# Second attention of a two-layer cross-attention kernel: all low parts of the probabilities on GpSimd, value banks copied out by VectorE, stacked operands through a pre-stacked scratch

## Chip, cores and metric

The kernel runs on one core of a Trainium2 chip. The metric is the device time of one execution in microseconds; a profiled execution gives the trace.

## What is computed

Two layers, each an attention and an MLP, for 4 batches of 512 tokens of width 512, 16 heads of 32. The change lies in the attention of the second layer alone:

```python
h = jnp.concatenate([x, latents], axis=1)               # 64 context rows + 512 latents
q = (latents @ q_w + q_b).reshape(b, k_len, NH, DH)
kv = (h @ kv_w + kv_b).reshape(b, p + k_len, NH, DH, 2)
kmat, v = (kv[..., 0], kv[..., 1])
attn = jnp.einsum('bkhd,bnhd->bhkn', q, kmat) / DH
attn = jnp.where(full_mask[:, None, None, :], attn, -jnp.inf)
attn = jax.nn.softmax(attn.astype(jnp.float32), axis=-1).astype(q.dtype)
attn_out = jnp.einsum('bhkn,bnhd->bkhd', attn, v).reshape(b, k_len, H)
attn_out = attn_out @ out_w + out_b + residual
```

## The kernel before

Every fp32 operand of a matmul is split into a high part, rounded to the matmul's type, and a low part, the difference from it; a product is made of three matmuls (high by high, high by low, low by high). For scores the split is stacked along the contraction: rows 0 to 31, 32 to 63 and 64 to 95 of `QS` hold high, high and low of a head's Q, those of `KS` high, low and high of its K, so that one matmul makes all three products. Row 96 is the mask, row 97 (`ROWMAX`) the row's maximum, which thus is subtracted by the same matmul.

The second attention (`attention1` on each engine) walks over 4 batches; a batch has 4 groups `c` of 4 heads, a group 20 steps: 4 heads by 5 key tiles (4 of 128 keys and one of 64 context keys). Steps are numbered `n` in the batch, `i` in the group. In step `n` TensorE issues

- `scores(n)`: the scores of step n, transposed (keys on partitions), into bank 4 or 5. At `i == 0` it waits for `maxed`, the DMA of the row of maxima of its group;
- `max_step`: one or two matmuls of scores of the *next* group, whose maxima over the keys VectorE takes (banks 2 and 3; steps 2 to 15 of a group). The first of each pair of heads waits for `stacked`, the loads of `QS` and `KS`;
- `values(n - 4)` (`LAG`): two matmuls of the value product of an earlier step, of the high part `ph` and the low part `pl` of its probabilities, into bank 6 or 7; one head's output is summed there over five steps. The low part it waits for by `p_lo` (VectorE) or `p_lo_pool` (GpSimd);
- a slice of the projections for the group after the next (`fillers`: Q, K, K of the context; in the second group also the transposes of the next batch's tokens).

ACT makes `exp(n)` twice from the bank, rounded into `ph` and in fp32 into `pf`, both rings of five (`PRING`); before it overwrites them it waits for the low part and the value matmul of step n - 5. The low part `pl = pf - ph` is made by GpSimd where `lo_by_pool(n)` says so (key tiles 1 and 3, and the context tile of even heads, 10 of 20 steps) and by VectorE (`lo_p`) otherwise.

When a head is finished, ACT (`o_out(h)`, one step behind the last value matmul) copies rows 0 to 64 of its bank into `sg`, VectorE (`o_sum(h)`) adds the high and the low half into `oa` and frees the bank, and SyncE (`sums(h)`) moves row 64, the sum of the probabilities, into `s16` by DMA.

SyncE issues all these DMAs in an order written out in `attention1.batch` for each group: the sums of the last head before, the parts of Q to the scratch `q_parts` in HBM (`parts(0, ...)`), a sums row, the parts of K (`parts(1, ...)`), the first half of the stacked loads (`pair(0)`, two heads), a sums row, the row of maxima (`max_row`, line 550), the second half of the stack (`pair(1)`), a sums row. The loads are for the group two further on. One half of a stack is three loads of 32 rows for Q and three for K (line 543), and for two of the four groups a mask row (line 546). The row of maxima comes from VectorE's join of two tables of maxima (line 1510), a transpose on TensorE (line 1950, issued in step 17) and a copy by VectorE (line 1517).

In the last batch, from step 40 on, GpSimd also loads and splits eight blocks of MLP weights, one every five steps (lines 696 to 711), in the same instruction stream as its low parts (line 841). In the last group of every batch it adds the bias row to four residual tiles (line 854).

Of the kernel before, what the change touches and what calls it, by code (L numbers as in the profile page):

```python
# [26 lines left out]
F32 = mybir.dt.float32  # L27
# [3 lines left out]
ACT = mybir.ActivationFunctionType  # L31
# [140 lines left out]
def lo_by_pool(i):  # L172

    j, t = STEPS[i % NSTEP]
    return t in (1, 3) or (t == TT and j % 2 == 0)
# [14 lines left out]
STACK = 16 * 13  # L190


def stack_count(c):
    return 16 * 7 if c < 2 else STACK
# [8 lines left out]
def program(nc, x, ctx, mask_bool, mask_int, w, x1, xm, x2, q_parts, k_parts, out):  # L203
# [4 lines left out]
    with es:  # L208
# [126 lines left out]
        pv_step = sem("pv_step")  # L335
        sg_ready = sem("sg_ready")
        o_free = sem("o_free")
# [110 lines left out]
        def _(sp):  # L448
# [77 lines left out]
            def attention1():  # L526
                src, dst = tokens(xm), tokens(x2)

                def parts(x, nb, c):

                    for half in range(2):
                        wait_apart(sp, (stacked[c % 2][half], at(0, nb, STACK, stack_count(c - 2) if c >= 2 else 0)))
                    sp.dma_start((q_parts, k_parts)[x][c % 2], (qt, kt)[x].bitcast(F32)).then_inc(parted[x][c % 2], 16)

                def stack(nb, c, half):

                    to = stacked[c % 2][half]
                    heads = slice(2 * half, 2 * half + 2)
                    for x, dst_, src_, order_ in ((0, QS, q_parts, (0, 0, 1)), (1, KS, k_parts, (0, 1, 0))):
                        wait_apart(sp, (parted[x][c % 2], at(0, nb, 32, 16 * (c // 2 + 1))))  # L540
                        rows_of = src_[c % 2].rearrange("(j p) h n -> p j h n", p=HD)
                        for r, part in enumerate(order_):
                            sp.dma_start(dst_[r * HD:(r + 1) * HD, c % 2, heads, :].bitcast(F32),
                                         rows_of[:, heads, part, :]).then_inc(to, 16)
                    if c < 2:
                        sp.dma_start(KS[ROWMASK:ROWMASK + 1, c % 2, heads, S:NK].bitcast(F32),
                                     kbias[0:1, 1, ds(nb * C, C)].bitcast(F32).unsqueeze(1).to_broadcast([1, 2, C]))\
                            .then_inc(to, 16)
# [8 lines left out]
                def batch(b, last):  # L557
                    def sums(h):
                        sp.wait_ge(sg_ready, at(0, b, H, h + 1))
                        sp.dma_start(s16[h:h + 1, :], sg[2 * HD:2 * HD + 1, h % 2, :])\  # L560
                            .then_inc(o_moved[h % 2], 16)
# [6 lines left out]
                    for c in range(G):  # L568
# [8 lines left out]
                        if last and c == G - 1:  # L577

                            wait_apart(sp, (pb_full, at(0, b, USES, use1(f"R{G - 1}", last) + 1)),
                                       (parted[0][1], at(0, b, 32, 32)), (parted[1][1], at(0, b, 32, 32)))  # L580
# [11 lines left out]
                        if ahead:  # L592
                            wait_apart(sp, (pb_free, at(0, b, USES, use1(f"{pre}KC{nc_}", last) + 1)))
                            parts(1, nb, nc_)
                            pair(0)
# [5 lines left out]
                        if ahead:  # L601
                            pair(1)
                        sums(HG * c + 2)
# [275 lines left out]
        def _(act):  # L879
# [167 lines left out]
            def attention1():  # L1047
# [5 lines left out]
                def hi(b, u, last=False, first=False):  # L1053

                    kind = u.lstrip("n")
                    if kind[0] in "QK":
# [3 lines left out]
                        if not (first and c == 0):  # L1060
                            wait_apart(act, (parted["QK".index(kind[0])][(c + 1) % 2],
                                             at(0, own, 32, 16 * ((c - 1) // 2 + 1) if c else 0)))
# [23 lines left out]
                def batch(b, last):  # L1086
# [19 lines left out]
                    def o_out(h):  # L1106
                        wait_apart(act, (pv_step, at(0, b, BSTEP, (h + 1) * (TT + 1))),
                                   (o_moved[h % 2], at(0, b, 128, 16 * (h // 2))), (o_free, at(0, b, H, h - 1)))
                        act.activation(sg[0:2 * HD + 1, h % 2, :], bank[6 + h % 2][0:2 * HD + 1, :], ACT.Copy)\
                            .then_inc(sg_ready, 1)  # L1110

                    for c in range(G):
                        at_step = {s0 + n: u for s0, n, u in fillers(c, last)}
                        for i in range(NSTEP):
# [4 lines left out]

                            h, t = divmod(n - LAG - 1, TT + 1)  # L1120
                            if t == TT and h >= 0:
                                o_out(h)
# [7 lines left out]
                    o_out(H - 1)  # L1130
# [58 lines left out]
        def _(dve):  # L1189
# [278 lines left out]
            def attention1():  # L1468
# [50 lines left out]
                def batch(b, last):  # L1519
# [10 lines left out]
                    def o_sum(h):  # L1530
                        j = h % HG
                        dve.wait_ge(sg_ready, at(0, b, H, h + 1))
# [611 lines left out]
```

## Time and profile before

| | before |
|---|---|
| median of 3 runs | 1864.66 us (1859.7 to 1866.77) |
| profiled execution | 1862.46 us, span 1860.6 |
| PE, DVE, ACT, POOL busy, share of the span | 88%, 54%, 38%, 29% |
| mean granted TensorE clock | 0.93 |
| second attention, first score to last value matmul | 766.4 to about 1436 us |

Engines are named as the profile names them: PE is TensorE, PEld its weight loads, DVE VectorE, ACT ScalarE, POOL GpSimd, SP SyncE (SPq its DMA queue). Times are microseconds from the span's start. In groups by line, "x" is a count, then the busy time, the mean of one, the idle time just before and what ended it. In the timeline, square brackets hold the idle time before an instruction and what released it. A shape is partitions x elements, output first.

### The profile page before, as it was taken

How to read it: one execution, taken by the hardware profiler on the slowest of the kernel's cores; microseconds unless marked ns; L12 is line 12 of the kernel's file. 1: busy time of each engine (PE TensorE's matmuls, PEld its weight loads, DVE VectorE, ACT ScalarE, POOL GpSimd, SP SyncE). 2: the span in 40 equal slices, each digit the busy share in tenths (PEclk: the TensorE clock that was granted, in tenths of full speed). 3: DMA queues.
4: the chain of work that ended last, by engine and by line, in shares of the span. 5: the costliest groups of instructions: out<-in, count | busy, mean ns of one | idle time of the engine just before them, and what ended most of it. 6: DMA issues, size and time to landing. Idle time of an engine off the chain costs nothing.

```text
span 1860.6 us, 23089 instructions
## 1 busy us (share of the span) xinstructions
PE 1642.2 (88%) x6993; PEld 1229.6 (66%) x6993; DVE 1009.4 (54%) x1612; ACT 703.4 (38%) x1260; POOL 541.9 (29%) x543
## 2 busy tenths in 40 slices
PE   5778887899999998888988898989886699999998
PEld 4667775667878786555665555655553477787886
DVE  3665565554333335667766766775787455334333
ACT  3433333431111111367556745663667232111111
POOL 2232245404040505133323422341358210404000
PEclk9788898999999998789988999998988799999999
DMA  5011023501010215223123223221221420101011
GB/s 176 1 40 63 23 91 100 177 1 46 0 45 0 91 70 186 68 83 112 61 72 94 87 61 109 65 91 61 95 84 46 151 81 1 46 0 45 0 41 50
DMA packets 60730, 126.13 MB, mean 68 GB/s; under 512 B 10397, under 2 KB 10722, under 8 KB 60642
## 3 DMA queue, kind: packets, MB, share of 16 engines
q1 hardware_dynamic: 53602, 102.08, 16.8%
q0 software_dynamic: 7040, 23.07, 4.1%
q8 instruction: 31, 0.51, 0.1%
q14 instruction: 57, 0.47, 0.1%
HBM read 90.25 MB, written 34.60 MB: 67 GB/s over the span
## 4 chain that ended last, share of the span: by engine, by line
PE 70%; DVE 14%; issue 6%; ACT 4%; DMA 3%; SPq 1%; POOL 0%; ACTq 0%; DVEq 0%; POOLq 0%
PE bank L2064 18%; PE bank L2052 17%; PE bank L1926 5%; DVE RA L1268 4%; PE bank L1961 3%; PE bank L1922 3%; PE bank L2023 3%; DVE FA L1501 3%; PE bank L1976 3%; PE bank L1977 2%; PE bank L1939 2%; PE bank L1748 2%; PE bank L1724 2%; PE bank L1943 2%; PE bank L1799 1%
## 5 line engine op out<-in xcount | busy, mean ns | idle before, releaser
L2064 PE MATMUL bank<-W,RA 128*128 128x512 f32 x1536 | 384.3, 402 | 25.3 <-DVE RA L1268 25.1
L2052 PE MATMUL bank<-RA,W 128*128 (+1 forms) x1536 | 374.7, 396 | 2.7 <-issue 2.3
L2064 PEld LDWEIGHTS bank<-W,RA 128*128 128x128 f32 x1536 | 290.3, 191 | 99.5 <-DVE RA L1268 31.2
L841 POOL TENSOR_TENSOR RA<-FA,RA 128x512 fp32r<-128x512 f32 (+1 forms) x160 | 216.0, 1354 | 423.9 <-ACT FA L1104 423.8
L2052 PEld LDWEIGHTS bank<-RA,W 128*128 128x128 f32 x1536 | 286.9, 188 | 74.9 <-issue 5.9
L1268 DVE TENSOR_TENSOR RA<-FA,RA 128x512 fp32r<-128x512 f32 (+2 forms) x308 | 274.7, 894 | 68.0 <-ACT FA L1104 54.5
L1160 ACT ACTIVATE FA<-bank,cols 128x512 f32<-128x512 f32 x128 | 88.2, 689 | 560.2 <-PE bank L2052 560.1
L1631 DVE CAST RA<-FA 128x512 fp32r<-128x512 f32 x128 | 62.5, 488 | 368.9 <-ACT FA L1160 368.7
L1103 ACT ACTIVATE RA<-bank 128x512 fp32r<-128x512 f32 (+1 forms) x320 | 192.4, 601 | 170.3 <-PE bank L1961 164.6
L1501 DVE TENSOR_REDUCE FA<-bank 128x1 f32<-128x512 f32 x256 | 169.1, 685 | 65.4 <-PE bank L1939 64.1
L1104 ACT ACTIVATE FA<-bank 128x512 f32<-128x512 f32 (+1 forms) x320 | 191.5, 599 | 0.0
L1961 PE MATMUL bank<-RA 98*128 98x512 f32 (+1 forms) x320 | 144.7, 454 | 37.5 <-DMA RA<-rows_ 29.7
L1926 PE MATMUL bank<-RA,W 128*128 128x512 f32 (+1 forms) x576 | 147.9, 375 | 5.3 <-DVE FA L1491 2.9
L1976 PE MATMUL bank<-RA 128*65 128x512 f32 (+1 forms) x320 | 140.5, 439 | 8.8 <-DVE RA L1268 5.2
L1268 DVE TENSOR_TENSOR RA<-bank,RA 128x512 fp32r<-128x512 f32 (+1 forms) x124 | 82.9, 680 | 114.2 <-ACT RA L1084 43.5
L1977 PE MATMUL bank<-RA 128*65 128x512 f32 (+1 forms) x320 | 135.1, 422 | 0.0
L1926 PEld LDWEIGHTS bank<-RA,W 128*128 128x128 f32 x576 | 99.7, 200 | 42.0 <-issue 14.1
L1961 PEld LDWEIGHTS bank<-RA 98*128 98x128 f32 (+1 forms) x320 | 62.8, 197 | 83.2 <-issue 45.6
L700 POOL TENSOR_TENSOR W<-raw,W 128x512 fp32r<-128x512 f32 (+1 forms) x88 | 110.2, 1252 | 7.4
L1661 DVE TENSOR_TENSOR FA<-bank,FA 128x512 f32 (+1 forms) x128 | 86.2, 689 | 37.8 <-PE bank L2064 37.2
L1939 PE MATMUL bank<-RA 97*128 97x512 f32 x256 | 100.3, 432 | 2.3 <-DVE FA L1501 1.8
L696 POOL TENSOR_SCALAR W<-raw 128x512 fp32r<-128x512 f32 (+1 forms) x88 | 55.1, 626 | 62.7 <-DMA raw<-in_L_xattn_mlp_w_dram 20.5
(149 smaller groups left out, 1838.1 us busy)
## 6 DMA issues: line engine op xcount, KB each, us to landing
RA<-k_parts SPq DMA_DIRECT2D x96, 144.0 KB
FA<-after_layer SPq DMA_DIRECT2D x12, 1024.0 KB, 6.2
RA<-q_parts SPq DMA_DIRECT2D x96, 128.0 KB
k_parts<-FA SPq DMA_DIRECT2D x16, 576.0 KB, 3.2
after_att<-FA SPq DMA_DIRECT2D x32, 256.0 KB, 2.1
q_parts<-FA SPq DMA_DIRECT2D x16, 512.0 KB, 2.7
raw<-in_L_xattn_mlp_w_dram POOLq DMA_DIRECT2D x32, 256.0 KB, 3.4
RA<-after_att SPq DMA_DIRECT2D x12, 512.0 KB, 8.6
```

Of the source, the lines that this page charges most:

```text
L841: pool.tensor_tensor(pl[0:m, r, :], pf[0:m, r, :], ph[0:m, r, :].bitcast(F32), ALU.subtract).then_inc(p_lo_pool, 1)
L1103: act.activation(ph[0:m, r, :], src, ACT.Exp, scale=SCALE1)
L1104: act.activation(pf[0:m, r, :], src, ACT.Exp, scale=SCALE1).then_inc(p_exp, 1)
L1268: dve.tensor_tensor(dst, src, hi.bitcast(F32), ALU.subtract).then_inc(sem_, 1)
L1501: dve.tensor_reduce(nm_main[:, TT * j + t:TT * j + t + 1], bank[2 + i % 2][:, :], AX_X, ALU.max, negate=True).then_inc(mm_free, 1)
L1926: op = pe.matmul(dst[:, 0:m], W[:, "QK".index(kind[0]), a, k, c * P:(c + 1) * P], src[:, d, k, :], start=start, stop=stop)
L1939: pe.matmul(bank[2 + i % 2][:, :], QS[0:ROWMAX, c % 2, j, t * P:(t + 1) * P], KS[0:ROWMAX, c % 2, j, 0:S], start=True, stop=True).then_inc ...
L1961: pe.matmul(bank[4 + n % 2][0:m, :], KS[0:ROWMAX + 1, c % 2, j, t * P:t * P + m], QS[0:ROWMAX + 1, c % 2, j, :], start=True, stop=True).th ...
L1976: pe.matmul(o, v, ph[0:m, n % PRING, :], start=(t == 0), stop=False)
L1977: pe.matmul(o, v, pl[0:m, n % PRING, :], start=False, stop=(t == TT)).then_inc(pv_step, 1)
L2052: op = pe.matmul(bank[FC1_BANK[i]][:, :], W[:, slot, a, k, i * P:(i + 1) * P], yT_[:, ds(b * (2 * KT * S) + (d * KT + k) * S, S)], start=( ...
L2064: op = pe.matmul(bank[4 + t][:, :], gs[:, a, i, t * P:(t + 1) * P], W[:, slot + 1, d, i, :], start=(i == 0 and a == 0 and d == 0), stop=(i ...
```

## The change

In the second attention:

- `lo_by_pool` is true for every step: GpSimd makes all 320 low parts, VectorE none;
- the copy of a finished head's bank into `sg` moves from ACT (`o_out` is removed) to VectorE, into `o_sum`, ahead of its addition;
- the scratch holds Q and K stacked already: `parts` writes three copies (high, high, low for Q; high, low, high for K) with three DMAs instead of both parts with one, and `stack` loads 96 rows with one DMA for Q and one for K instead of three each. The counts that are waited for follow (48 instead of 16 on `parted`, 3 or 2 loads of 16 on `stacked` where there were 7 or 6);
- in SyncE's order `pair(0)` moves behind `sums(HG * c + 1)` and `max_row`, and `pair(1)` behind `sums(HG * c + 2)`.

```diff
 def lo_by_pool(i):
     j, t = STEPS[i % NSTEP]
-    return t in (1, 3) or (t == TT and j % 2 == 0)
+    return True
...
-STACK = 16 * 13
+STACK = 16 * 5
 def stack_count(c):
-    return 16 * 7 if c < 2 else STACK
+    return 16 * 3 if c < 2 else STACK
...
                     for half in range(2):
                         wait_apart(sp, (stacked[c % 2][half], at(0, nb, STACK, stack_count(c - 2) if c >= 2 else 0)))
-                    sp.dma_start((q_parts, k_parts)[x][c % 2], (qt, kt)[x].bitcast(F32)).then_inc(parted[x][c % 2], 16)
+                    to = (q_parts, k_parts)[x][c % 2]
+                    for r, part in enumerate(((0, 0, 1), (0, 1, 0))[x]):
+                        sp.dma_start(to[:, r, :, :], (qt, kt)[x][:, part, :].bitcast(F32)).then_inc(parted[x][c % 2], 16)
...
-                    for x, dst_, src_, order_ in ((0, QS, q_parts, (0, 0, 1)), (1, KS, k_parts, (0, 1, 0))):
-                        wait_apart(sp, (parted[x][c % 2], at(0, nb, 32, 16 * (c // 2 + 1))))
-                        rows_of = src_[c % 2].rearrange("(j p) h n -> p j h n", p=HD)
-                        for r, part in enumerate(order_):
-                            sp.dma_start(dst_[r * HD:(r + 1) * HD, c % 2, heads, :].bitcast(F32),
-                                         rows_of[:, heads, part, :]).then_inc(to, 16)
+                    for x, dst_, src_ in ((0, QS, q_parts), (1, KS, k_parts)):
+                        wait_apart(sp, (parted[x][c % 2], at(0, nb, 96, 48 * (c // 2 + 1))))
+                        sp.dma_start(dst_[0:3 * HD, c % 2, heads, :].bitcast(F32),
+                                     src_[c % 2, heads].rearrange("j r p n -> (r p) j n")).then_inc(to, 16)
...
                             parts(1, nb, nc_)
-                            pair(0)
                         sums(HG * c + 1)
                         if not (last and c == G - 1):
                             u = f"R{c + 1}" if c + 1 < G else "nR0"
                             wait_apart(sp, (pb_free, at(0, b, USES, use1(u, last) + 1)))
                             max_row(b if c + 1 < G else b + 1, (c + 1) % G)
                         if ahead:
+                            pair(0)
+                        sums(HG * c + 2)
+                        if ahead:
                             pair(1)
-                        sums(HG * c + 2)
...
-                    def o_out(h):
-                        wait_apart(act, (pv_step, at(0, b, BSTEP, (h + 1) * (TT + 1))),
-                                   (o_moved[h % 2], at(0, b, 128, 16 * (h // 2))), (o_free, at(0, b, H, h - 1)))
-                        act.activation(sg[0:2 * HD + 1, h % 2, :], bank[6 + h % 2][0:2 * HD + 1, :], ACT.Copy)\
-                            .then_inc(sg_ready, 1)
...
                     def o_sum(h):
                         j = h % HG
+                        dve.wait_ge(pv_step, at(0, b, BSTEP, (h + 1) * (TT + 1)))
+                        wait_apart(dve, (o_moved[h % 2], at(0, b, 128, 16 * (h // 2))))
+                        dve.tensor_copy(sg[0:2 * HD + 1, h % 2, :], bank[6 + h % 2][0:2 * HD + 1, :]).then_inc(sg_ready, 1)
                         dve.wait_ge(sg_ready, at(0, b, H, h + 1))
...
-    parts = [nc.dram_tensor(n, (2, P, 2, m), F32, kind="Internal").ap() for n, m in (("q_parts", S), ("k_parts", NK))]
+    parts = [nc.dram_tensor(n, (2, HG, 3, HD, m), F32, kind="Internal").ap() for n, m in (("q_parts", S), ("k_parts", NK))]
```

## Rows read from the trace of the kernel before

**Rows 1.** Busy time by stretch (window, length, then each engine, clock, DMA)
```profile
948.40:1087.50 139.10, 121.61 (x530) 81.26 (x530) 103.65 (x159) 98.53 (x191) 57.43 (x43) 0.94 0.29 90
...
981.90:1020.80 38.90, 35.18 (x149) 23.95 (x149) 25.47 (x40) 25.35 (x50) 12.85 (x10) 0.88 0.24 72
```

**Rows 2.** Waits of TensorE, 766 to 1440: total us, times, longest
```profile
PE bank L1961 <- DMA RA<-rows_: 29.7, 11, 3.9
PE bank L1943 <- DVE FA L1501: 23.1, 27, 2.0
...
PE bank L1903 <- DVE FA L1491: 7.9, 6, 1.6
```

**Rows 3.** VectorE by line and shape, 766 to 1440
```profile
L1501 DVE TENSOR_REDUCE FA<-bank 128x1 f32<-128x512 f32 x240 | 158.3, 685 | 64.4 <-PE bank L1939 63.5
L1268 DVE TENSOR_TENSOR RA<-FA,RA 128x512 fp32r<-128x512 f32 x140 | 144.0, 1031 | 46.8 <-ACT FA L1104 41.4 <-ACT RA L1144 4.9
L1533 DVE TENSOR_TENSOR FA<-bank,FA 32x512 f32<-32x512 f32 x64 | 43.8, 684 | 3.9 <-ACT FA L1109 2.1
```

**Rows 4.** ACT's copy of a value bank: ns min/median/max, first and last start
```profile
L1109 ACT ACTIVATE FA<-bank x64: 582/584/682, 785.7 to 1436.4; 65x512 f32<-65x512 f32 x64
```

**Rows 5.** Timeline of low parts: start, us, engine, line, operation, count
```profile
954.79 2.53 POOL L841 TENSOR_TENSOR RA<-FA,RA 128x512 fp32r<-128x512 f32 x2 [0.78 <-ACT FA L1104]
...
958.82 1.29 POOL L841 TENSOR_TENSOR RA<-FA,RA 128x512 fp32r<-128x512 f32 x1 [1.51 <-ACT FA L1104]
958.89 1.77 DVE L1268 TENSOR_TENSOR RA<-FA,RA 128x512 fp32r<-128x512 f32 x1
...
1433.73 1.26 POOL L841 TENSOR_TENSOR RA<-FA,RA 128x512 fp32r<-128x512 f32 x1
```

**Rows 6.** Timeline of SyncE's DMA queue at a group's end
```profile
1047.90 1.63 SPq L543 DMA_DIRECT2D RA<-q_parts  x3
...
1052.63 0.53 SPq L560 DMA_DIRECT2D FA<-FA  x1
1053.35 0.56 SPq L551 DMA_DIRECT2D RA<-rows_  x1
1054.17 1.30 SPq L543 DMA_DIRECT2D RA<-q_parts  x3
```

**Rows 7.** Timeline of VectorE and TensorE at group ends and starts
```profile
1049.52 0.28 DVE L1517 CAST rows_<-bank 16x128 fp32r<-16x128 f32 x1
...
1055.29 0.76 PE L1961 MATMUL bank<-RA 98*128 98x512 f32 x1 [3.85 <-DMA RA<-rows_]
...
1020.86 0.47 PE L1961 MATMUL bank<-RA 98*128 98x512 f32 x1 [0.41 <-DMA RA<-rows_]
...
1023.50 0.40 PE L1939 MATMUL bank<-RA 97*128 97x512 f32 x1
...
1372.45 0.77 PE L1961 MATMUL bank<-RA 98*128 98x512 f32 x1 [3.31 <-DMA RA<-rows_]
```

**Rows 8.** Busy time in one slice, with the DMA share and GB/s last
```profile
1058.00:1059.00 1.00, 1.00 (x4) 0.81 (x3) 0.01 (x1) 0.64 (x2) 0.19 (x1) 0.50 0.56 124
```

**Rows 9.** The page's DMA issues: count, KB each, us to landing
```profile
k_parts<-FA SPq DMA_DIRECT2D x16, 576.0 KB, 3.2
```

**Rows 10.** GpSimd by line, 1370.4 to 1435.1, the last batch's second half
```profile
L841 POOL TENSOR_TENSOR RA<-FA,RA 128x512 fp32r<-128x512 f32 (+1 forms) x21 | 29.8, 1428 | 5.0 <-ACT FA L1104 5.0
L700 POOL TENSOR_TENSOR W<-raw,W 128x512 fp32r<-128x512 f32 x8 | 11.7, 1464 | 0.7
L854 POOL TENSOR_TENSOR FA<-FA,brow 128x512 f32<-128x512 f32 x4 | 6.5, 1617 | 0.0
L696 POOL TENSOR_SCALAR W<-raw 128x512 fp32r<-128x512 f32 x8 | 5.0, 629 | 4.0 <-DMA raw<-in_L_xattn_mlp_w_dram 3.8
L711 POOL DMA_DIRECT2D raw<-in_L_xattn_mlp_w_dram x7 | 4.1, 584 | 0.0
```

**Rows 11.** The join of maxima: ns min/median/max, first and last start
```profile
L1510 DVE TENSOR_TENSOR FA<-FA x16: 175/175/178, 763.3 to 1398.8; 128x16 f32<-128x16 f32 x16
```

## What the change will do to the time

> **What bounds the kernel now.** The second attention is the stretch from 766 to 1440 us: four batches of 80 steps, 20 steps to a group of four heads, then the batch's tail (value projections, normalising, output projection). I read it in four views. The first is the table of busy time by stretch [rows 1]: the reader is to see that in the 139.1 us of one batch's steps TensorE is busy 121.6, VectorE 103.7 and GpSimd only 57.4. TensorE is thus the engine nearest to full, but part of its busy time is slow time: the group from 981.9 shows a granted clock of 0.88. Of the two levels (1.0 and 0.5 of full, 2.4 and 1.2 GHz) that is 24% of 38.9 us, 9.3 us, at the lower one; at full clock the same work would have taken some 4.6 us less.
>
> The second view, who TensorE waited for [rows 2], tells what interrupts it: the row maxima that come by DMA (29.7 us in 11 waits, always the first score of a group), and VectorE (23.1 and 7.9 us) where a bank of maxima or of a projection was not yet drained. The third, VectorE by line and shape [rows 3], says why VectorE is late: its low parts of the probabilities (both inputs in SBUF) take 1031 ns on the mean, while instructions of the same size that read PSUM take 685. The timeline shows the cause [rows 5]: a GpSimd low part begins at 958.82 for 1.29 us, a VectorE one at 958.89 needs 1.77 and ends 0.55 after GpSimd's. The fourth view is the timeline of the queues at a group's end [rows 6, 7].
>
> **The change, part by part.**
>
> *Low parts.* VectorE gives up 160 of 320, 40 a batch; at 1.0 us (128 rows, by [rows 3]) that is 40 us of its 103.7. GpSimd takes them. Two back to back took 2.53 us [rows 5], so 1.27 each when VectorE doesn't interfere, and nothing of VectorE's steps would now have two large SBUF inputs. 80 a batch are 101.6 us, and four residual additions of the same size 5.1: 106.7 us in 139. By the step, GpSimd needs 1.27 (1.52 in a batch's last group) where a step lasts 1.74 on the mean (139.1/80). A step's low part is due four steps later, about 6 us; score, two exponentials and 1.27 make some 3. So in the first three batches GpSimd keeps up, and what hides the longer instruction is the lag of four steps. The cover is thin in a group's last four steps, which carry no maxima and run at ACT's pace of about 1 us: there GpSimd falls back 4 x 0.3 us and recovers at the next group's start. Taken as nothing to +4 us in all.
>
> *Copying out.* The 64 copies of the value banks move from ACT (584 ns each, 37 us, [rows 4]) to VectorE. The trace has no such copy on VectorE; nearest is its addition that reads the same bank, 684 ns [rows 3], so 11 us a batch. VectorE's sum: 103.7 - 40 + 11 = 75 of 139 us. The copy waits for the value matmul and for the earlier sums row to have left by DMA; behind it in VectorE's queue stand the next maxima, for which TensorE would wait. Both signals belong to work two or more steps older, so the wait should be over on arrival. Value: 0, between 0 and +5.
>
> What TensorE gains: of the 31 us that it waited for VectorE [rows 2] I take two thirds, 20, since VectorE goes from 75% to 54% busy. Bounds: 5 (waits set by bursts of two maxima, not by load) to 35 (all of it and some clock).
>
> *SyncE's queue.* Before, at the group's end at 1047.9, the queue issued three Q stack loads, waited for the K scratch, issued three K loads and the mask rows, then a sums row at 1052.63, and only at 1053.35 the row of maxima [rows 6], though VectorE had that row at 1049.80 (1049.52 + 0.28) [rows 7]. TensorE stood for 3.85 us until 1055.29. After, the queue reaches the maxima before the stack: issue at about 1050.0, and the score could start 1.94 later as before (1055.29 - 1053.35), at 1051.9 instead of 1055.3. TensorE's own work ended at 1051.44, so some 0.5 us of wait stay.
>
> The first half of the stack, moved past that row, now starts at about 1050.6 instead of 1047.9. The second half in the trace was issued at 1054.17 [rows 6], and its bytes ended in the slice 1058 to 1059, which is 0.56 busy, so about 4.4 us later [rows 8]. The first half would land at 1055.0. Who waits for it: the first matmul of maxima in the next group, which stood 2.6 us behind the group's first score at full clock (1020.86 to 1023.50, [rows 7]); so it is due at 1054.5. A new wait of about 0.5 us takes the place of 3.85, a net gain of 2.9. Of the 11 waits three or four (the group in which the tokens are transposed, 0.41 at 1020.86) have nothing to give, and lose up to 0.5. Eight give on the mean 2.6: 20 us. Bounds: nothing (the stack lands 3 us later than that) to 30. The second half moves past one sums row alone, and its due time is six or more steps off: 0.
>
> *Scratch and stack DMAs.* Q and K are written to the scratch in three copies rather than two parts (3 issues for 1, half as many bytes more), and each stack load is 1 issue for 3 with the same bytes. One K write of 576 KB landed in 3.2 us [rows 9]; 864 KB would need 4.8 by proportion, but it is issued four or five steps ahead of the stack in its new place, and the buffer that it frees is refilled a group later. Value 0; bounds -2 to +6. The same at the start of the stage: two more issues, hidden by VectorE's set-up: 0 to +2.
>
> *The last batch* is where GpSimd has no room. From step 40 on it also splits eight weight blocks. The window from 1370.4 to 1435.1 [rows 10] shows 29.8 us of low parts in 21 instructions, 11.7 and 5.0 of splits, 6.5 of residual, 4.7 of DMA issue (seven in 4.1, and an eighth alike), 3.8 of waiting for the first block, and only 5.0 us idle. After: 40 x 1.27 = 50.8; 8 x 1.27 = 10.2; 5.0; 4 x 1.27 = 5.1; 4.7; 3.8: together 79.6 us. Before, step 40's score stood at 1372.45 [rows 7]; its low part, now the first in the line, can start some 1.7 us later (0.77 and two ACT instructions of about 0.5). 1374.1 + 79.6 = 1453.7, against 1435.0 for the last GpSimd low part before (1433.73 + 1.26, [rows 5]). Nothing covers that: values, sums and the tail follow it. +19 us. Bounds: +12 (half the first block's wait and the start hidden) to +28 (1428 and 1464 ns an instruction as now, [rows 10]).
>
> The Trainium skill (GPSIMD Engine Reference, section Engine selection) speaks against the move: for an elementwise operation on two inputs it wants VectorE, GpSimd being about twice as slow. The rows agree on the instruction, 1.27 against about 0.69, but which engine has the time to spare decides here, and that is GpSimd outside the last 40 steps.
>
> **Sum**, against the profiled execution (1862.46, span 1860.6, 2.2 below the median of 1864.66): -20 (waits for VectorE) - 20 (group ends) + 19 (last batch) = -21, 1841.5 for such an execution, or 1844 by the median.
>
> **Rivals.**
> 1. *GpSimd becomes the pace in all four batches* (slower). If a low part takes 1.62 us, as the residual additions do on the mean among VectorE's traffic [rows 10], a batch's 84 instructions take 136 us, and with some 3 us before its first low part as long as the steps take now (139): the gains of all batches are gone, and the last 40 steps cost +28: 1892. It decides from about 1.5 us an instruction, where 84 of them and the 3 us pass the 129 that the steps need after the gains. Against it: back to back they took 1.27, and the interfering instructions leave.
> 2. *The stack load takes the place of the row of maxima* (no change). If the one large load lands 3 us later than computed, each group waits at its first maxima as long as it did at its first score: the 20 us of the group ends are gone, 1864. For it: the K half must wait for three scratch copies, 4.8 us by proportion.
> 3. *More comes free* (faster). VectorE's waits go wholly, and TensorE, with no idle of 3 us at group ends, keeps its clock: 5 us more a batch: 1864 - 20 - 20 + 19 - 20 = 1823.
> 4. *GpSimd blocks the joining of maxima* (no change). The join reads two SBUF tiles and stands on the path to the row of maxima. In the trace it took 175 to 178 ns all 16 times [rows 11], never blocked; but GpSimd was half idle. With GpSimd always running, each join could wait the rest of an instruction, up to 1.27, on the mean 0.6 us, 15 times, and VectorE's queue with it: +10 us, 1854. The Trainium skill (SBUF — State Buffer, section SBUF: two separate sides) says that such an instruction and a GpSimd one exclude each other for their whole length; the pair at 958.8 agrees.
>
> **How the numbers follow.** Chances: forecast 0.49, rival 1 0.12, rival 2 0.20, rival 3 0.13, rival 4 0.06. Predicted: 1844. The range takes rivals 3, 4 and 2 with some of their own width: 1820 to 1872; rival 1 and the ends stay out. About 0.5% (9.3 us) is what a measurement of this kernel can tell: faster is below 1855, with the forecast and rival 3, 0.62; same, rivals 2 and 4, 0.26; slower, rival 1, 0.12.
>
> **What would show it.** Right: TensorE's waits for the row of maxima fall from 29.7 to under 10 us; its waits for VectorE's reductions to under 12; VectorE shows no instruction of over 1 us in the steps; the low parts on GpSimd come at 1.27; the step part of a middle batch takes 126 to 130 us instead of 139; the last 40 steps of the last batch take 78 to 84 us instead of 63. A wait for a stack load of over 2 us at every group speaks for rival 2, a GpSimd instruction mean of over 1.5 us for rival 1, joins of over 0.5 us for rival 4. Wrong would be a step part that stays at 139 with GpSimd named as what TensorE waits for.

## The result, and the profile after

The kernel became slower. Its median is 1963.74 us (1962.45 to 1967.65, 4 runs), that of the kernel before, run beside it, 1862.88 (1859.7 to 1866.77): a ratio of 1.0544, with a 95% interval of 1.0517 to 1.0571. The forecast was 1844 within 1820 to 1872. The profiled execution has a span of 1961.4 us, 100.8 more than before, and a mean granted clock of 0.896 where it was 0.930.

I split the span at the first score of the stage, at the last batch's first score and its step 40, and at the last value matmul:

| us | start to first score | first three batches | last batch, 40 steps | last 40 steps | behind it | span |
|---|---|---|---|---|---|---|
| before | 766.4 | 536.9 | 69.1 | 63.5 | 424.7 | 1860.6 |
| after | 782.7 | 592.8 | 77.8 | 81.6 | 426.5 | 1961.4 |

The loss lies in every batch (56 us in the first three) and at the start (16), and only 18 of it in the last 40 steps, where GpSimd was expected to be late. The first view is who TensorE waited for, from 760 to 1560 us (total us, times, longest), which answers [rows 2]:

```profile
PE bank L1953 <- DMA RA<-rows_: 94.2, 13, 9.9
PE bank L1968 <- POOL RA L841: 16.7, 12, 2.2
...
PE bank L1942 <- DVE FA L1499: 7.1, 12, 1.7
...
PE bank L1935 <- DVE FA L1490: 3.1, 12, 0.3
```

The wait for VectorE's reductions (now line 1935, 23.1 us before) is gone. The wait for the row of maxima, which the change was to shorten, went from 29.7 us in 11 to 94.2 in 13. The second view shows one of the 13, in the timeline of SyncE's queue (start, us, line, operation, count), which answers [rows 6]:

```profile
1005.68 2.17 SPq L535 DMA_DIRECT2D k_parts<-FA  x3
1007.98 1.78 SPq L560 DMA_DIRECT2D FA<-FA  x1
1009.95 0.59 SPq L551 DMA_DIRECT2D RA<-rows_  x1
1010.88 0.35 SPq L543 DMA_DIRECT2D RA<-q_parts  x1
1019.64 0.32 SPq L543 DMA_DIRECT2D RA<-k_parts  x1
```

and the matching line of TensorE (in brackets the idle time before, and what ended it):

```profile
1020.05 0.77 PE L1953 MATMUL bank<-RA 98*128 98x512 f32 x1 [9.93 <-DMA RA<-rows_]
```

The order is the one intended: the row of maxima is issued at 1009.95, ahead of the stack. But it lands 10.1 us after its issue, not 1.9 as in [rows 6, 7]; and the K half of the stack, which waits for the three scratch copies issued from 1005.68, is issued at 1019.64, 14.0 us after them. One copy of 576 KB, two thirds of these bytes, took 3.2 us before [rows 9]. K's loads wait for the copies in the program; the row of maxima waits for nothing once it is issued, and still landed only when the copies had. The third view is the table of busy time by stretch, with the columns of [rows 1], within that wait, just behind it, and over the first three batches; below it three rows to compare with, two of the kernel before (behind the 3.85 us wait of [rows 7], and its first three batches) and one of the kernel after with the old scratch, an experiment below (its first three batches):

```profile
1016.00:1017.00 1.00, 0.00 (x0) 0.00 (x0) 0.00 (x0) 0.00 (x0) 0.00 (x0) 0.50 0.25 86
...
1020.00:1025.00 5.00, 4.95 (x12) 3.28 (x13) 0.30 (x1) 2.80 (x6) 2.55 (x2) 0.50 0.82 211
1025.00:1030.00 5.00, 5.00 (x24) 3.43 (x23) 2.38 (x4) 2.76 (x6) 3.08 (x3) 0.98 0.19 46
...
782.70:1375.40 592.70, 476.54 (x1956) 320.61 (x1957) 285.24 (x464) 305.04 (x573) 320.43 (x252) 0.86 0.28 85
```

```profile
1055.30:1060.30 5.00, 5.00 (x13) 3.38 (x14) 1.06 (x2) 2.86 (x6) 1.49 (x2) 0.55 0.62 164
...
766.40:1303.30 536.90, 473.30 (x1956) 317.95 (x1957) 360.07 (x536) 325.84 (x621) 180.42 (x132) 0.91 0.26 81
```

```profile
762.30:1288.10 525.80, 471.44 (x1957) 315.73 (x1958) 284.67 (x464) 302.46 (x573) 319.34 (x252) 0.92 0.26 83
```

The last but one column is the share of 16 DMA engines: while every compute engine stands and the copies alone are under way, it is 0.25 (0.26 from 1014 to 1018), four engines of sixteen. The column before it is the clock: TensorE stands, and the first 5 us of the next group run at the lower level (0.50), with 12 matmuls where the next 5 us see 24. That looks like a second cost, but most of it isn't new: behind the 3.85 us wait the first 5 us had a clock of 0.55 and 13 matmuls. Over three batches TensorE was busy for 476.5 us, 473.3 before: of the 55.8 us more, 3.2 are busy time. Against the kernel after with the old scratch, which has every other part of the change, it is 5.1 of 66.9; the rest is standing.

Why four engines: the scratch before is one contiguous block of 128 rows; after, `to[:, r, :, :]` picks one of three parts of each of four heads, so that the HBM side of a copy is 4 blocks of 32 rows that can't be merged. The Trainium skill (DMA: Bandwidth & Descriptors, section "Why a DMA increments its semaphore by 16 and not by 1") says that a DMA is spread over the largest number up to 16 that divides the slowest dimension of both sides: 16 for 128 rows, 4 for 4 blocks. The share of 0.25 agrees; the experiments test it at 4 and at 2 on the kernel before.

At the stage's start and in the batch tails the same thing shows. The first Q and K copies, in the queue's timeline after and then before:

```profile
721.49 1.81 SPq L535 DMA_DIRECT2D q_parts<-FA  x3
723.49 8.67 SPq L535 DMA_DIRECT2D k_parts<-FA  x3
735.52 0.35 SPq L543 DMA_DIRECT2D RA<-q_parts  x1
```

```profile
724.62 0.34 SPq L533 DMA_DIRECT2D q_parts<-FA  x1
725.15 0.32 SPq L533 DMA_DIRECT2D k_parts<-FA  x1
729.60 1.26 SPq L543 DMA_DIRECT2D RA<-q_parts  x3
```

From the first copy's issue to the first stack load are 14.0 us instead of 5.0, and issuing K's copies alone held the queue for 8.67. In the three tails between batches VectorE's reciprocal waits 14.5 us in all for the sums rows (last row of the next view; in the fourth it waits for none), and each of them takes 37.5 us from the last value matmul to the next first score, where it took 31.1 to 31.2. VectorE by line and shape, which answers [rows 3]:

```profile
L1523 DVE COPY FA<-bank 65x512 f32<-65x512 f32 x64 | 43.5, 679 | 34.7 <-PE bank L1969 30.0 <-DMA FA<-FA 4.6
L1499 DVE TENSOR_TENSOR FA<-FA 128x16 f32<-128x16 f32 x16 | 5.6, 348 | 0.5
L1563 DVE RECIPROCAL FA<-FA 16x512 f32<-16x512 f32 x4 | 13.4, 3344 | 14.6 <-DMA FA<-FA 14.5
```

GpSimd did what was forecast; its low parts (ns minimum, median, maximum), answering [rows 5]:

```profile
L841 POOL TENSOR_TENSOR RA<-FA,RA x320: 1251/1281/1455, 786.3 to 1533.1; 128x512 fp32r<-128x512 f32 x128, 64x512 fp32r<-64x512 f32 x32
```

### The profile page after: what moved, and what is told of

Its sections match the earlier page's. It is cut to its first block, busy times and chain, and to the rows that moved or that the text cites. A ratio compares the mean times of both kernels' runs of the same rounds, so it can differ in the third digit from the quotient of the medians.

```text
span 1961.4 us, 23079 instructions
## 1 busy us (share of the span) xinstructions
PE 1660.7 (85%) x6993; PEld 1237.9 (63%) x6993; DVE 903.9 (46%) x1516; ACT 677.1 (35%) x1196; POOL 725.0 (37%) x703
## 4 chain that ended last, share of the span: by engine, by line
PE 65%; DVE 10%; DMA 9%; issue 6%; ACT 4%; POOL 2%; SPq 2%; DVEq 0%; POOLq 0%; ACTq 0%
PE bank L2056 17%; PE bank L2044 16%; PE bank L1918 6%; DMA RA<-rows_ 5%; PE bank L1953 3%; PE bank L1968 3%; PE bank L1931 3%; PE bank L2015 3%; PE bank L1969 2%; DVE RA L1257 2%; DMA k_parts<-FA 2%; PE bank L1716 2%; PE bank L1740 2%; POOL RA L841 2%; PE bank L2009 1%
## 5 line engine op out<-in xcount | busy, mean ns | idle before, releaser
L841 POOL TENSOR_TENSOR RA<-FA,RA 128x512 fp32r<-128x512 f32 (+1 forms) x320 | 406.8, 1282 | 338.8 <-ACT FA L1104 334.0
L2056 PEld LDWEIGHTS bank<-W,RA 128*128 128x128 f32 x1536 | 291.5, 192 | 100.0 <-DVE RA L1257 31.1
L2044 PEld LDWEIGHTS bank<-RA,W 128*128 128x128 f32 x1536 | 287.1, 188 | 75.2 <-issue 6.2
L1953 PE MATMUL bank<-RA 98*128 98x512 f32 (+1 forms) x320 | 148.8, 467 | 100.3 <-DMA RA<-rows_ 94.2
L1968 PE MATMUL bank<-RA 128*65 128x512 f32 (+1 forms) x320 | 147.0, 459 | 16.9 <-POOL RA L841 16.7
L1969 PE MATMUL bank<-RA 128*65 128x512 f32 (+1 forms) x320 | 140.9, 440 | 0.0
L1918 PEld LDWEIGHTS bank<-RA,W 128*128 128x128 f32 x576 | 104.4, 208 | 51.3 <-issue 14.0
L1257 DVE TENSOR_TENSOR RA<-FA,RA 128x512 fp32r<-128x512 f32 (+1 forms) x148 | 113.4, 768 | 13.0 <-ACT RA L1133 6.5
L1653 DVE TENSOR_TENSOR FA<-bank,FA 128x512 f32 (+1 forms) x128 | 86.2, 689 | 37.5 <-PE bank L2056 37.0
L1968 PEld LDWEIGHTS bank<-RA 128*65 128x65 f32 (+1 forms) x320 | 48.4, 151 | 55.3 <-POOL RA L841 37.1
```

The lines of the kernel that those rows point to most:

```text
L841: pool.tensor_tensor(pl[0:m, r, :], pf[0:m, r, :], ph[0:m, r, :].bitcast(F32), ALU.subtract).then_inc(p_lo_pool, 1)
L1257: dve.tensor_tensor(dst, src, hi.bitcast(F32), ALU.subtract).then_inc(sem_, 1)
L1918: op = pe.matmul(dst[:, 0:m], W[:, "QK".index(kind[0]), a, k, c * P:(c + 1) * P], src[:, d, k, :], start=start, stop=stop)
L1953: pe.matmul(bank[4 + n % 2][0:m, :], KS[0:ROWMAX + 1, c % 2, j, t * P:t * P + m], QS[0:ROWMAX + 1, c % 2, j, :], start=True, stop=True).th ...
L1968: pe.matmul(o, v, ph[0:m, n % PRING, :], start=(t == 0), stop=False)
L1969: pe.matmul(o, v, pl[0:m, n % PRING, :], start=False, stop=(t == TT)).then_inc(pv_step, 1)
```

## The experiments

Theory A: the loss is the shape of the scratch copies. Theory B: it is GpSimd, whatever the shape. Theory C: it is SyncE's new order. Every ratio below is against the kernel before, run on the same chip, with its 95% interval. No kernel leaves out part of the work.

**Low parts alone.** The kernel before with

```diff
-    return t in (1, 3) or (t == TT and j % 2 == 0)
+    return True
```

> The kernel before with one part of the change: GpSimd makes all 320 low parts; copies, scratch, stack loads and queue order as before. Theory A (the loss comes from the scratch copies, which the trace of after shows at about a quarter of the DMA engines: K's three copies are issued at 1005.68 and the stack load behind them can go at 1019.64, 14 us, while the DMA share stands at 0.13 to 0.3 and 50 to 110 GB/s): this part is harmless, some 20 us gained from VectorE and some 19 lost in the last batch, 1850 to 1870. Theory B (GpSimd's 1.28 us instructions are the pace): most of the 100 us, 1930 or more, with TensorE's waits for L841 in tens of us. Theory C (the new queue order is the loss): as A.

1848.66 us, ratio 0.9926 (0.9904 to 0.9948). Who TensorE waited for:

```profile
PE bank L1961 <- DMA RA<-rows_: 29.0, 10, 3.7
...
PE bank L1943 <- DVE FA L1501: 2.9, 11, 0.3
```

Alone, this part gains 15 us, a little more than I expected. By stretch (span 1849.0) the first three batches took 513.2 us instead of 536.9 and the last batch's first 40 steps 65.0 instead of 69.1; its last 40 took 80.2 instead of 63.5. So -28 and +17: GpSimd isn't the cause of the loss. Theory B falls. Not all of the 24 us in three batches is waiting: TensorE's busy time there fell from 473.3 to 463.5 us, at a granted clock of 0.92 instead of 0.91.

**The shape alone, on the kernel before.** One spare row in the scratch behind each 32, so that the same 128 rows and bytes are 4 blocks of 32; order and everything else stay (the loads' addresses follow, in a line that is left out here):

```diff
-    (q_parts, k_parts)[x][c % 2], (qt, kt)[x].bitcast(F32)
+    (q_parts, k_parts)[x][c % 2][:, 0:HD, :, :], (qt, kt)[x].bitcast(F32)
-    (2, P, 2, m)
+    (2, HG, HD + 1, 2, m)
```

> The kernel before with nothing of the change but the shape of its scratch copies: the scratch has one unused row behind each head's 32, so the same one copy of the same bytes goes out as 4 x 32 rows instead of 128. Theory A (a copy whose outermost size is 4 goes over 4 of the 16 DMA engines): the K copy lands in 9 to 10 us instead of 3.2 (864 KB took 14 us in the changed kernel, 576 KB is two thirds), each group's end waits some 6 us longer, 11 times, and the clock falls with it: 1925 to 1950. Theories B and C, and any theory in which the bytes or the number of copies matter: no change, 1860 to 1870.

1967.37 us, ratio 1.0564 (1.0533 to 1.0595): a loss as large as that of the whole change, from rows that nobody reads, and more than I had expected. SyncE's queue at a group's end and the wait of TensorE:

```profile
1055.01 0.57 SPq L533 DMA_DIRECT2D k_parts<-FA  x1
...
1065.39 1.24 SPq L543 DMA_DIRECT2D RA<-k_parts  x3
```

```profile
PE bank L1961 <- DMA RA<-rows_: 95.4, 13, 11.1
```

From the K copy to the stack's K loads are 10.4 us. In this order the row of maxima is late because SyncE stands ahead of it; in the kernel after, though it stands in front, because the copies' data do. The wait is the same, 95.4 and 94.2. The clock costs more here: the first three batches took 616.8 us instead of 536.9, and 15 of these 80 are TensorE's busy time (488.5 for 473.3, granted clock 0.86 for 0.91).

**The two controls.** A spare row behind each 64 (2 blocks, first edit), and one behind all 128 (still one block, second edit):

```diff
-    (2, P, 2, m)
+    (2, 2, 2 * HD + 1, 2, m)
...
+    (2, P + 1, 2, m)
```

> The kernel before with the unused scratch row behind each pair of heads, so that the one copy of the same bytes goes out as 2 x 64 rows. If the outermost size sets how many DMA engines take part (4 x 32 made K's copy last 10.4 us where 128 rows took 3.2): about twice 10.4, 19 to 21 us for K, some 10 us more at each of 15 group ends than with 4 x 32, 2090 to 2160. If it is the break in the addresses or the odd row: as with 4 x 32 or better, 1930 to 1970.

> The kernel before with one unused scratch row behind all 128, so that the copy stays 128 rows and only the scratch is larger. If the outermost size is the cause: 1855 to 1872, as before. If the scratch's size or place in HBM were: slower.

With the row at the end 1862.59 us, ratio 0.9993 (0.9976 to 1.0009); the K copy lands in 3.2 us:

```profile
k_parts<-FA SPq DMA_DIRECT2D x16, 576.0 KB, 3.2
```

With 2 blocks 2041.69, ratio 1.0963 (1.091 to 1.1016). Its queue, its DMA share (0.13, two engines of sixteen) and its wait:

```profile
1087.13 0.55 SPq L533 DMA_DIRECT2D k_parts<-FA  x1
...
1101.10 1.24 SPq L543 DMA_DIRECT2D RA<-k_parts  x3
```

```profile
1094.00:1098.00 4.00, 3.30 (x17) 1.49 (x15) 1.57 (x3) 4.00 (x9) 2.25 (x2) 1.00 0.13 53
```

```profile
PE bank L1961 <- DMA RA<-rows_: 142.8, 13, 15.1
```

So padding costs nothing. And one break in the block costs more than three: what counts is the number of blocks, not that of the breaks. The size was again off: I expected twice the time of 4 blocks; from the K copy to the stack's K loads are 14.0 us against 10.4.

**The change with the scratch and stack loads of before.** Low parts, copying out and order as after:

```diff
-                    to = (q_parts, k_parts)[x][c % 2]
-                    for r, part in enumerate(((0, 0, 1), (0, 1, 0))[x]):
-                        sp.dma_start(to[:, r, :, :], (qt, kt)[x][:, part, :].bitcast(F32)).then_inc(parted[x][c % 2], 16)
+                    sp.dma_start((q_parts, k_parts)[x][c % 2], (qt, kt)[x].bitcast(F32)).then_inc(parted[x][c % 2], 16)
...
-    (2, HG, 3, HD, m)
+    (2, P, 2, m)
```

> The changed kernel with the scratch and the stack loads of before (one copy of 128 rows with both parts, three loads of 32 rows for each half); GpSimd's low parts, VectorE's copy and the new queue order stay. Theory A: K lands in 3.2 us again, the row of maxima goes out ahead of the stack: what the prediction forecast, 1835 to 1860. Theory B: 1930 or more. Theory C: 1930 or more.

1862.40 us, ratio 1.0007 (0.9975 to 1.0038). The scratch's shape thus costs 1963.7 - 1862.4 = 101 us here, and 1967.4 - 1862.6 = 105 on the kernel before: theory A. Theory C falls too as the cause of the 101 us, since the new order is still in this kernel. But 1862 is just outside what I expected; without the shape the rest of the change gains nothing, though its low parts alone gain 15. Its waits, then the queue and the wait at one group's end:

```profile
PE bank L1931 <- DMA RA<-k_parts: 17.4, 8, 2.5
...
PE bank L1953 <- DMA RA<-rows_: 7.4, 9, 2.5
...
PE bank L1931 <- DMA RA<-rows_: 6.8, 3, 2.3
```

```profile
1039.89 0.55 SPq L551 DMA_DIRECT2D RA<-rows_  x1
1040.79 1.27 SPq L543 DMA_DIRECT2D RA<-q_parts  x3
1042.18 1.29 SPq L543 DMA_DIRECT2D RA<-k_parts  x3
1043.62 0.68 SPq L546 DMA_DIRECT2D RA<-rows_  x1
```

```profile
1046.39 0.50 PE L1931 MATMUL bank<-RA 97*128 97x512 f32 x1 [2.24 <-DMA RA<-rows_]
```

The first score (line 1953) hardly waits any more: 2.5 of its 7.4 us are at the stage's very first score, as before. Here it starts at 1041.83, 1.94 us after the row's issue, as before. The first matmul of maxima (line 1931) waits for the stack instead, K's loads or, where there is one, the mask row behind them (line 546, which the view names `rows_` too): 17.4 + 7.4 + 6.8 = 31.6 us, about what the row of maxima alone cost before (29.7).

**The stacked scratch, written in blocks of 32 rows.** The kernel after with each scratch copy cut by head: 12 issues of 32 rows, each contiguous, instead of 3 of 4 blocks:

```diff
-                        sp.dma_start(to[:, r, :, :], (qt, kt)[x][:, part, :].bitcast(F32))...
+                        for j in range(HG):
+                            sp.dma_start(to[j, r, :, :], (qt, kt)[x][j * HD:(j + 1) * HD, part, :].bitcast(F32))...
```

> The changed kernel with each scratch copy of 128 rows cut in four copies of 32 rows (12 issues for 3, the same bytes to the same places). Theory A: copies of 32 rows use all engines, K lands in 4 to 5 us; 12 issues take SyncE some 4.5 us instead of 2.2; waits for the row of maxima fall from 94 us to 10 to 30; 1845 to 1875. Theory B (GpSimd) and theory C (queue order): 1940 to 1965, since nothing of theirs changes.

1884.38 us, ratio 1.0119 (1.0075 to 1.0163): 79 of the 101 us come back with the same bytes in the same layout, a little less than I expected. The rest is 22 us over the run just above; the only things that differ are the 12 issues and half as many bytes more to the scratch, against one load instead of three. The 12 issues keep the queue for 5.46 us ahead of the row of maxima, and TensorE's waits for that row are 33.9 us, more than the 10 to 30 expected:

```profile
1012.38 5.46 SPq L536 DMA_DIRECT2D k_parts<-FA  x12
```

**Order alone, copying out alone**, on the kernel before. The edits are those of the diff above, `pair` moved in SyncE's order and `o_out` moved to VectorE.

> The kernel before with only SyncE's order changed (both halves of the stack behind the row of maxima and a sums row). If the order trades one wait for another (in the run with the old scratch the waits for the row of maxima were 4.9 us instead of 29, and 24.2 us of waits for stack loads stood in their place): 1860 to 1870, no difference beyond 0.5%. If the order gains what the prediction took for it: 1843. If the order is what made that run 13 us slower than low parts alone: 1872 to 1880.

> The kernel before with only the copy of a finished head's bank moved from ACT to VectorE. VectorE still makes its half of the low parts, so it gets 11 us a batch on top of 103.7: if the copy is hidden, 1860 to 1868; if VectorE's queue is close to its limit there, 1870 to 1885, with TensorE's waits for reductions above 23 us.

The order: 1875.84, ratio 1.0063 (1.0032 to 1.0094). The copy: 1881.26, ratio 1.0073 (1.004 to 1.0105). Both lose. Waits with the order alone, then with the copy alone:

```profile
PE bank L1940 <- DMA RA<-k_parts: 19.7, 8, 3.8
PE bank L1962 <- DMA RA<-rows_: 8.3, 10, 2.5
PE bank L1940 <- DMA RA<-rows_: 7.1, 3, 2.5
```

```profile
PE bank L1935 <- DVE FA L1490: 25.1, 38, 2.0
PE bank L1953 <- DMA RA<-rows_: 25.0, 12, 3.8
```

The order moves 21 us away from the first score (29.7 to 8.3) and puts 27 at the stack loads. What the copy costs on a VectorE that still makes half of the low parts isn't in one row of waits: that for a bank of maxima is only 2 us longer, in 38 instead of 27 pieces. It stands in TensorE's busy time: 488.9 us over the first three batches where it was 473.3, at a granted clock of 0.89 instead of 0.91; that is 15.6 of the 17.1 us by which they are longer. What lowered the clock wasn't tested.

**Each of the two beside the low parts.**

> The kernel before with GpSimd making all low parts and VectorE making the copies out; scratch, stack loads and order as before. The copy alone cost some 14 us, on a VectorE that still made its low parts. If that price is VectorE's load, it goes with the low parts: within 3 us of low parts alone, 1846 to 1853. If the copy costs by its place (ACT no longer paced by it, SyncE's sums rows later): 1858 to 1866.

> The kernel before with GpSimd making all low parts and the new order of SyncE's queue; copies, scratch and stack loads as before. The order alone cost some 12 us. If the stack loads behind the row of maxima are what costs, it costs the same here: 1858 to 1864, with 20 to 27 us of waits for stack loads. If it was VectorE's load that made the order dear: 1840 to 1850.

Low parts and copy: 1848.39, ratio 0.9935 (0.9914 to 0.9956), what the low parts gain alone (0.9926). Low parts and order: 1861.16, ratio 0.9995 (0.9969 to 1.002). So the copy is free once VectorE is relieved, and the order costs about 12 us on either base. Its waits:

```profile
PE bank L1940 <- DMA RA<-k_parts: 18.9, 8, 2.9
...
PE bank L1940 <- DMA RA<-rows_: 8.3, 3, 3.0
PE bank L1962 <- DMA RA<-rows_: 8.0, 10, 2.5
```

Over the whole stage they come to 35.2 us against 29.0 for low parts alone, 6 of the 12. The rest is again in TensorE's busy time: over the first three batches, 16.5 us longer in the profiled executions (529.7 for 513.2), it is 474.5 us instead of 463.5, at a granted clock of 0.91 instead of 0.92. Why stays open.

**The last 40 steps shared as before**, with the low parts on GpSimd everywhere else:

```diff
+    return not last or i < 2 * NSTEP or t in (1, 3) or (t == TT and j % 2 == 0)
```

> The kernel before with GpSimd making all low parts except in the last 40 steps of the last batch, where the old division between VectorE and GpSimd stays. If the 16 to 18 us that those 40 steps took longer (80.2 us with all low parts on GpSimd, 63.5 before) come from GpSimd's weight splits beside 40 low parts: 63 to 66 us again for them, 1830 to 1838 in all. If they come from something else (clock, norm work on VectorE): as the run with all low parts on GpSimd, 1845 to 1855.

1835.57 us, ratio 0.9844 (0.9807 to 0.9882). The first three batches took 513.8 us (513.2 with low parts alone), the last 40 steps 63.6, as before: the cost at the end and the gain elsewhere are two separate terms.

**Only the K loads pass the row of maxima.** That kernel, and in SyncE's order only the half that waits for the K scratch moved behind `max_row`; Q's three loads stay ahead and `pair(1)` stays where it was:

```diff
                             parts(1, nb, nc_)
-                            pair(0)
+                            pair(0, (0,))
                         sums(HG * c + 1)
...
                         if ahead:
+                            pair(0, (1,))
                             pair(1)
```

> As the run with the low parts shared at the end, and with the first half of the stack divided in SyncE's order: its Q loads stay where they were, its K loads (which wait for the scratch) go behind the row of maxima. If issue time and the wait for K's copy ahead of the row of maxima are what the 29 us of waits are made of: waits for that row fall to about 15, stack waits stay under 8, 1820 to 1833. If the stack then is as late as in the new order: no better than the run without it.

1811.99 us, ratio 0.9719 (0.9676 to 0.9762): faster than both kernels, 23.6 us faster than without the split on the same chip, and below the 1820 to 1833 that I expected. The queue and the wait:

```profile
1022.52 0.33 SPq L533 DMA_DIRECT2D k_parts<-FA  x1
1023.19 1.63 SPq L545 DMA_DIRECT2D RA<-q_parts  x3
1024.94 0.51 SPq L562 DMA_DIRECT2D FA<-FA  x1
1025.71 0.56 SPq L553 DMA_DIRECT2D RA<-rows_  x1
1026.38 1.45 SPq L545 DMA_DIRECT2D RA<-k_parts  x3
```

```profile
PE bank L1965 <- DMA RA<-rows_: 10.2, 9, 2.5
```

While the K copy lands, the queue issues what doesn't need it: Q's loads, a sums row, the row of maxima. K's loads then start 3.9 us after the copy's issue, with nothing left to wait for. The wait for the row falls from 28.4 us to 10.2, and those for the stack loads are 1.3 us in all. TensorE's busy time over the first three batches falls with it, from 463.9 us to 455.8, at a granted clock of 0.95 instead of 0.92: 8 of the 21 us gained there, which the expectation had left out. Two things differ from the order of the change, that Q's loads stay ahead and that `pair(1)` isn't moved; which of them counts more wasn't separated.

## Why the prediction was wrong, step by step

*What bounds the kernel*: right. TensorE, interrupted by the row of maxima at group ends and by VectorE's drained banks. Both waits moved when their causes were touched.

*Low parts*: right in the mechanism, and too careful by 8. Forecast -20 in the steps, all from waits; low parts alone gave 536.9 - 513.2 = 24 in three batches and 4 in the last one's first half. But 10 of the 24 are TensorE's busy time at a better clock, which the forecast had kept for its third rival: that the size is near is in part luck. 1.27 us an instruction was forecast, 1.28 came; the wait for reductions was to fall below 12 us and fell to 2.9. The cover held: TensorE's 16.7 us of waits for GpSimd's low parts all lie in the last batch, none of them before its step 40.

*Copying out*: right in the kernel as a whole (0: 1848.39 against 1848.66), at 679 ns where 684 was taken. That it rests on the other part of the change wasn't said: alone it costs some 14 to 18 us.

*The last batch*: right. +19 forecast with 78 to 84 us for its last 40 steps; 81.6 after, +18; +17 with low parts alone.

*Scratch and stack DMAs*: this step failed, and it is the result. From run to run the medians go 1848.66 (low parts), 1848.39 (with the copy), 1862.40 (with the order), 1963.74 (with the scratch and its stack loads). "864 KB would need 4.8 by proportion" scaled a time by bytes although the pattern of the copy changed with them: 128 contiguous rows became 4 blocks of 32. Measured were 14.0 us from the first of the three copies to the load that waits for them. And "it is issued four or five steps ahead of the stack ... Value 0" looked for who waits for the copy itself, and not for who queues behind it: at a group's end the row of maxima, in the tail the sums rows, at the start the first stack. The bounds of -2 to +6 stood against +101: 63 more of TensorE's waiting at group ends (94.2 against 31.6 with the old scratch), 20 at the start (782.7 against 762.3) and 19 in the three tails (37.5 us each against 31.1). In these tails VectorE's reciprocal waits 14.5 us for the sums rows, and with the old scratch it doesn't wait. The start's own "0 to +2" failed by the same step.

*SyncE's order*: this step failed too, by 32 to 34 us, hidden under the other. Forecast -20 with a new stack wait of 0.5 us a group; with three loads a half it is +12 to +14 (1861.16 against 1848.66, 1862.40 against 1848.39), and the new waits come to 27 us in eleven, up to 3.8 each (19.7 and 7.1 with the order alone). The first score's wait fell as forecast, to 8.0 us. The mis-sized term is the landing of a half of the stack: "about 4.4 us later" was read from the DMA share of one slice, where the bytes end. In the run with the old scratch, in the same group, it is 5.6 us from the first load's issue to the end of TensorE's wait for the half (1040.79 to 1046.39). The half also starts 0.9 us behind the row's issue instead of 0.6, and is due 0.3 earlier behind the first score (1044.15 against 1041.83): a wait of 2.24 us where 0.5 was forecast. TensorE's longer busy time (11 us, above) wasn't in the forecast at all. With the single loads of the change and a scratch that is written at full width the order was not tried: three copies that each spread over 16 engines into that layout were not found, and twelve (1884 us) bring a cost of their own.

*The rivals*: the second had the right mechanism, the stack load in the place of the row of maxima, and priced it at 1864: the run with the old scratch gave 1862.40, with 31.6 us of such waits for 29.7. That the two agree is partly luck, since the gain of the low parts and the price of the order were both larger than taken. It named the three scratch copies as what the stack must wait for, but again at 4.8 us. The first, GpSimd as the pace, is out (1.28 us an instruction). The fourth, the join blocked by GpSimd, shows in small: with low parts alone 15 of 16 joins took 782 to 901 ns, over its sign of 0.5 us, and TensorE's waits for them are 5 us in 12; they are 7.1 in the kernel after, where three joins took 1090 ns and the others 174 to 207. (Its 1854 was counted as no change, though the prediction's own line for faster is 1855.) The third, a clock that gains, came in part: over the first three batches 0.92 instead of 0.91 with low parts alone, and 0.95 with the split pair. Over the whole run of low parts alone it is 0.923 where it was 0.930 before, since the last 40 steps lose more: there it is 0.65 where it was 0.83.

*The tell-tales*: the row of maxima below 10 us came out at 94.2 and named the failed step at once; a middle batch, from its first score to the next one's, took 197.8 us (979.70 to 1177.51) instead of 177.3, and not for GpSimd. The range ended at 1872, since the cost of a copy pattern that the trace of before does not show had been bounded by bytes alone.

## What to carry to other kernels

A DMA's time isn't its bytes alone: before scaling one by size, write down both sides' shapes after merging what is contiguous, and compare the outermost size with that of the row that you scale from; a copy of the same 576 KB landed in 3.2 us with 128 rows, and held the loads that wait for it until 10.4 and 14.0 us after its issue with 4 blocks and 2 blocks. A slow transfer is charged to whatever is queued behind its wait or its data, here a row of 2048 numbers (8 KB) on which every group starts, so ask of each wait in a queue who stands behind it. And where an issue order is to be improved, try first to move only the transfer that waits: here K's loads alone gave -24 us, where the whole block that holds them gave +12 (on other bases, and with `pair(1)` moved too).

## What was unexpected of the hardware

- Fewer engines hurt small transfers behind them as much as the large one: the row of maxima, issued 4 us behind the copies, landed after 10.1 us instead of 1.9.
- With two engines the loads behind the copy went out 14.0 us after its issue, with four 10.4 us, not half of it. Other traffic in the same stretch may be the reason; that stayed open.
- The pattern also costs issue time: one K copy keeps SyncE's queue for 0.33 us with 128 rows, 0.57 with 4 blocks, 0.55 with 2.
- The join of two 128x16 tables on VectorE, beside a GpSimd that is nearly always at work, was held up: 894 ns in the median with low parts alone, and 1090 ns in three of 16 in the kernel after (348 on the mean), where all 16 took 175 to 178 before [rows 11].
- Behind a stop of 9.93 us TensorE's clock was hardly lower than behind one of 3.85: 0.50 and 0.55 in the first 5 us, with 12 and 13 matmuls. But the clock isn't free: with the shape alone, with the copy alone and with the order beside the low parts, TensorE's busy time over three batches was 11 to 16 us longer than in the kernels without them.
